# Width transform of a spectral block: one matmul over 128 rows, or two tiles of 64 rows into two PSUM banks

## The reference

```python
def _L0_conv_ref(x, w1, b1, w2, b2, bias_w, bias_b):
    bias = x @ bias_w.T + bias_b
    xb = x.reshape(B, H, W, nb, bs)
    xf = jnp.fft.rfftn(xb, axes=(1, 2), norm='ortho')
    xr, xi = (xf.real, xf.imag)
    r1 = jax.nn.relu(_block_mul(xr, w1[0]) - _block_mul(xi, w1[1]) + b1[0])
    i1 = jax.nn.relu(_block_mul(xr, w1[1]) + _block_mul(xi, w1[0]) + b1[1])
    r2 = _block_mul(r1, w2[0]) - _block_mul(i1, w2[1]) + b2[0]
    i2 = _block_mul(r2, w2[1]) + _block_mul(i1, w2[0]) + b2[1]
    out = jnp.fft.irfftn(jax.lax.complex(r2, i2), s=(H, W), axes=(1, 2), norm='ortho')
    return out.reshape(B, H, W, C) + bias
...
x = x + _L0_conv_ref(_gn(x), ...)
```

## Time and profile before

| | |
|---|---|
| runs, us | 493.98, 493.12, 493.60 (median 493.6) |
| the profiled execution | 493.3 us, span of its instructions 491.4 us |
| PE busy / weight loads busy | 462.8 us (94%) / 402.8 us (82%) |
| DVE busy | 327.0 us (67%) |
| ACT busy | 238.1 us (48%) |
| granted TensorE clock, mean | 0.982 of 2.4 GHz |

### The profile page before, as it was taken

How to read it: one execution, slowest core, us unless ns; L and a number is a source line. 1 busy time by engine, 2 the same in 40 slices (tenths; PEclk the granted TensorE clock), 3 DMA queues, 4 the chain that set the end, 5 groups by cost and what they waited for, 6 DMA issues and landing times.

```text
span 491.4 us, 15722 instructions
## 1 busy us (share of the span) xinstructions
PE 462.8 (94%) x6728; PEld 402.8 (82%) x6728; DVE 327.0 (67%) x769; ACT 238.1 (48%) x567; POOL 15.3 (3%) x16
## 2 busy tenths in 40 slices
PE   5476899999999999999999999999999999999996
PEld 5374688799888898799988998889987998887884
DVE  3695975578566884668756784668756785668524
ACT  3733483257542674247632683337732575425510
POOL 0030700000000000000000000000000000000000
PEclk9679999999999999999999999999999999999999
DMA  7640000250005100070003300070002500030003
GB/s 219 172 148 2 1 1 13 81 201 1 3 35 191 69 1 3 33 259 1 3 23 134 137 1 3 35 256 3 3 13 87 193 3 2 35 129 3 1 3 129
DMA packets 11637, 32.37 MB, mean 66 GB/s; under 512 B 4196, under 2 KB 5904, under 8 KB 11568
## 3 DMA queue, kind: packets, MB, share of 16 engines
q1 hardware_dynamic: 11568, 31.36, 18.1%
HBM read 15.63 MB, written 12.58 MB: 57 GB/s over the span
## 4 chain that ended last, share of the span: by engine, by line
PE 87%; DVE 5%; issue 3%; ACT 3%; DMA 1%; POOL 0%; DVEq 0%; SPq 0%; POOLq 0%; ACTq 0%
PE bank L521 87%; DVE r L989 1%; DVE rsum L982 1%; DMA x_sb<-in_x 1%; ACT y L813 1%; ACT junk L801 1%; DVE o_sb L1004 0%; DVE z L914 0%; ACT rho L848 0%; DVE extreme L1124 0%; ACT r L823 0%; DVE biasw L914 0%; ACT junk L804 0%; ACT z L833 0%; DVE rho L914 0%
## 5 line engine op out<-in xcount | busy, mean ns | idle before, releaser
L521 PE MATMUL bank<-w2s,rho 96*64 96x96 f16 (+1 forms) x3072 | 119.9, 247 | 0.0
L521 PEld LDWEIGHTS bank<-w2s,rho 96*64 96x64 f16 (+1 forms) x3072 | 107.9, 125 | 11.4 <-issue 11.3
L521 PE MATMUL bank<-biasw,y 128*128 128x384 f16 x576 | 105.4, 330 | 0.1
L521 PEld LDWEIGHTS bank<-biasw,y 128*128 128x128 f16 x576 | 78.6, 146 | 14.0 <-issue 0.2
L818 ACT ACTIVATE g<-bank 128x384 f16<-128x384 f32 x64 | 31.1, 485 | 98.3 <-PE bank L521 98.3
L996 DVE SCALAR_TENSOR_TENSOR g<-g,bank 128x384 f16<-128x384 f16 x64 | 35.4, 553 | 56.9 <-ACT g L818 56.9
L521 PE MATMUL bank<-w1R,y 128*128 128x192 f16 (+3 forms) x768 | 59.5, 228 | 4.4 <-ACT y L813 3.2
L833 ACT ACTIVATE z<-bank 128x384 f16<-128x384 f32 x72 | 35.3, 490 | 56.0 <-PE bank L521 56.0
L521 PEld LDWEIGHTS bank<-tab,x_sb 128*128 128x128 f32 x384 | 51.1, 201 | 9.1 <-issue 6.0
L521 PE MATMUL bank<-tab,x_sb 128*128 128x128 f32 x384 | 52.7, 285 | 6.0 <-DMA x_sb<-in_x 5.8
L914 DVE SCALAR_TENSOR_TENSOR z<-bank,z 128x384 f16<-128x384 f32 x72 | 39.7, 557 | 25.7 <-ACT z L833 24.7
(11 more groups left out here) (103 smaller groups left out, 421.5 us busy)
## 6 DMA issues: line engine op xcount, KB each, us to landing
x_sb<-in_x SPq DMA_DIRECT2D x16, 768.0 KB, 6.5
out<-o_sb SPq DMA_DIRECT2D x14, 768.0 KB, 4.1
y<-y SPq DMA_DIRECT2D x24, 128.0 KB, 2.7
out<-o_sb SPq DMA_DIRECT2D x8, 192.0 KB, 1.9
tab<-in_tab SPq DMA_DIRECT2D x1, 642.0 KB, 4.7
o_sb<-in_bias_wt SPq DMA_DIRECT2D x4, 144.0 KB, 2.7
b1s<-in_b1h SPq DMA_DIRECT2D x1, 384.0 KB, 5.2
o_sb<-in_w SPq DMA_DIRECT2D x2, 144.0 KB
```

Of the source, the lines that this page charges most:

```text
L521: return nc.tensor.matmul(o, lhsT, rhs, start=start, stop=stop, **kw)
```

## The change

Each float32 matmul of `p1` becomes two of half the size. One takes partitions 0 to 63 of `x_sb` (one pair of rows) as its stationary operand and 64 columns of the table, the other partitions 64 to 127 and their own 64 columns. They are row tiles of 64 rows in the array, and write two different banks. The zeros of the table are gone, and it is half as wide (TAB "width" 128 instead of 256 columns per partition).

An item now fills two banks: `y_bank[0:2]` for even `m`, `b_bank[0:2]` for odd `m`. `y_copy` becomes two activations of 256 columns each. The waits move with the banks: item 0 takes over the wait on `o_ready`, item 1 waits until `z` units 0 to 7 of the current image are evacuated, and `p4` takes its banks in another order.

```diff
-    width = by_unit(width.reshape(2, 128, 2, 4, 4, 4)).reshape(2, 128, 2, 64)
+
+    width = by_unit(width.reshape(2, 128, 2, 4, 4, 4)).reshape(2, 2, 64, 32, 2, 2)
+    width = np.stack([width[:, j, :, :, j, :] for j in range(2)], axis=1)
...
         def rho_bank(j, more):
-            return (*b_bank, *(y_bank if more else c_bank[0:2]))[j % 5]
+            return ((b_bank[2], *y_bank, *b_bank[0:2]) if more else (*b_bank, *c_bank[0:2]))[j % 5]
+
+
+        p1_banks = (y_bank, b_bank[0:2])
...
                 if m == 0 and not first:
                     pe.wait_ge(dve_step, NSTEP * (b - 1) + VAR_READ)
+                    pe.wait_ge(o_ready, 8 * b)
                 if m == 1 and not first:
-                    pe.wait_ge(o_ready, 8 * b)
+                    pe.wait_ge(zh_ready, 9 * b - 1)
+                    pe.wait_ge(zl_ready, 9 * b - 1)
                 if ct == 0:
                     pe.wait_ge(x_loaded[p][h], (b - p) * 8 + 16)
                 for i in range(4):
                     t = 4 * h + i
-                    src = x_sb[p][:, t, 128 * ct:128 * ct + 128]
-                    last = mm(y_bank[m % 2][:, 128 * i:128 * i + 128], src, width[:, 0 if t == 0 else 1, :], True, True)
+                    for j in range(2):
+                        rows = slice(64 * j, 64 * j + 64)
+                        last = mm(p1_banks[m % 2][j][:, 64 * i:64 * i + 64], x_sb[p][rows, t, 128 * ct:128 * ct + 128],
+                                  width[rows, 0 if t == 0 else 1, :], True, True)
                 last.then_inc(y_prod, 1)
...
-                    if j == 3 and more:
+                    if j in (1, 2) and more:
+                        pe.wait_ge(y_raw, Y_ITEMS * (b + 2) - 1)
+                    elif j == 3 and more:
                         pe.wait_ge(y_raw, Y_ITEMS * (b + 2))
                     elif j in (3, 4) and not more:
                         pe.wait_ge(spec_sum, 9 * b + 4 + j)
+                    elif j == 0 and more:
+                        pe.wait_ge(zh_ready, 9 * b + 9)
+                        pe.wait_ge(zl_ready, 9 * b + 9)
...
-                nc.scalar.activation(yraw[:, ct, :, :].rearrange("k a (m t) -> k (a m) t", t=TILES)[:, :, 4 * h:4 * h + 4],
-                                     y_bank[m % 2][:, :].rearrange("k (t m) -> k m t", t=4), ACT.Copy).then_inc(y_raw, 1)
+                columns = yraw[:, ct, :, :].rearrange("k a (c j x t) -> k (a c) j x t", j=2, x=2, t=TILES)
+                nc.scalar.activation(columns[:, :, 0, :, 4 * h:4 * h + 4],
+                                     p1_banks[m % 2][0][:, 0:256].rearrange("k (t c x) -> k c x t", t=4, x=2), ACT.Copy)
+                nc.scalar.activation(columns[:, :, 1, :, 4 * h:4 * h + 4],
+                                     p1_banks[m % 2][1][:, 0:256].rearrange("k (t c x) -> k c x t", t=4, x=2), ACT.Copy).then_inc(y_raw, 1)
```

More of the change, by code:

```diff
@@ L159 @@
 TABW = TAB16W = 0
-for _name, _wide in (("width", 256), ("own", 128), ("block3", 128), ("const", 64), ("rowscale", 1), ("coef", 5)):
+for _name, _wide in (("width", 128), ("own", 128), ("block3", 128), ("const", 64), ("rowscale", 1), ("coef", 5)):
     TAB[_name] = (TABW, TABW + _wide)
@@ L176, in put @@
         table[:a.shape[0], place[name][0]:place[name][1]] = a.reshape(a.shape[0], -1)
-    put("width", width.reshape(2, 128, 128).transpose(1, 0, 2))
+    put("width", width.reshape(2, 128, 64).transpose(1, 0, 2))
     put("height", H_SCALE * hgt.transpose(1, 0, 2))
```

## The result

The changed kernel takes 509.4 us (median of 4 runs, 508.39 to 509.84) against 493.8 (median of 4, 493.12 to 494.31) before: ratio 1.031, 95% interval 1.0298 to 1.0325. It is slower by 15.6 us, inside the stated range (492 to 522) and over the forecast of 501.9 by 7.5.

A forecast was written before the change was run, and what follows sets the result against it. PE, busy 94% of the span and unbroken in the steady chain, was taken as the bound. 36 items x 0.23 us = 8.3 us, start and first image nothing: 493.3 + 8.3 = 501.6, median 501.9 us; range 492 to 522.

The forecast's parts named there:

- The load sets the pace, side by side, nothing gained: In an item: 0.111 us per load sets the pace, both row tiles load together, 0.89 us as before.
- Two changes of shape per item: Between an item and its p3 neighbours: 0.25 us going in, 0.14 coming out, 0.23 us more per item.
- The start's six items stand in a row, with no change of shape: nothing: First group of items at the start: no added time; shorter table also taken as nothing, with 0.3 us as bound.
- So the first image pays nothing: First image's p3 stage: its six items cost nothing because PE waits there anyway; 1.4 us without that cover.
- The cover by DVE's waits: First image: PE's waits for rsum, 4.69 us before 46.40 and 1.05 before 55.85, hide the items' added time.
- A: The forecast case: tile loads side by side, two changes of shape per item; 499 to 508 us, chance 0.55.
- C: Rival: within a row tile a load isn't hidden under that tile's matmul; 512 to 522 us, chance 0.16.
- ACT and the banks: In the p3 stage: two copies take 0.78 us, ACT's 1.29 us fits a 1.61 us turn, PE doesn't wait for banks.
- E: Rival: a tile's load goes by the weights it holds, 0.056 us a pass; 483 to 487 us, chance 0.10.

The follow-up runs named there:

- e1: The kernel before with 64 moving columns instead of 128 in its width matmuls, half the transform left out: 495.0 us, ratio 1.0019.
- e2: The changed kernel with the tile of rows 0 to 63 alone, 8 loads and 8 matmuls per item instead of 16: 508.6 us.
- e3: The kernel before with the changed banks, waits, order of p4 and two activations per copy, its matmuls whole: 494.6 us, ratio 1.001.
- e4: The changed kernel with four tiles of 64 rows by 64 channels, 64 columns loaded and 64 moving: 490.3 us, ratio 0.9931.
- e5: The kernel before with two column tiles of 64 channels, all 128 rows and 128 moving columns: 502.7 us, ratio 1.0171.

## Why the prediction was right, and where it was off

- **The load sets the pace, side by side, nothing gained**: right, and shown three ways, by the loads two by two in the trace, by e1 and by e2. It rested on the 3-column matmuls, which any argument from moving columns would have missed.
- **Two changes of shape per item**: right in kind, and the size was near. Forecast 0.23 us an item, measured 0.26 (1.58 / 6). Going in is 0.26 us, as read from the earlier trace rows: the last `p3` matmul starts 0.16 us behind 111.96, at 112.12, the item at 112.38. Going out was taken as 0.14 from float16 tiles. Here the last matmul starts at 112.38 + 1.11 - 0.27 = 113.22 and the unit behind it at 113.42, 0.20 us. Float32 tile matmuls last 0.27 us in the trace, the float16 ones 0.207, which would account for it; no run tests that. In between, from the first matmul to the last, are 0.84 us where 8 x 0.111 = 0.89 stood, so two small errors partly cancel. 36 items make 9.5 us where 8.3 stood.
- **"The start's six items stand in a row, with no change of shape: nothing"**: wrong by 3.6 us in the two profiles, at least 2.3 against the others. The step counted the loads at their pace at full clock, which the kernel before reaches half way through this group. It never asked whether the changed items would reach it too. They don't. Nor did the shorter table bring the data earlier.
- **"So the first image pays nothing"**: wrong by 2.6 us. The cover by DVE's waits was read rightly: item 1 starts at 47.88, behind a wait of 3.46 us for `z`, and PE still waits 0.40 us for `rsum` behind it, with 1.05 us for the last unit gone. What followed ran at half clock for 17 us instead of 3.4. These two terms are 6.2 of the 7.4 us by which the forecast fell short, and the steady images the other 1.2. A's own range (499 to 508) had no room for them; the stated one had, for the sake of C, which did not happen. That the measured time lies in it is luck: the mechanism of A accounts for 9.5 of the 15.7 us, and the rest has a cause that no rival names.
- **ACT and the banks**: right. Each copy takes 0.38 us, and e3 puts the whole part at 0.5 us or less.
- **E, the faster side**: the reason against it held. A float32 load of 64 rows still passes at 0.11 us; it goes by its columns. The Trainium skill, TensorEngine Tiling, section Theoretical Speedup, has up to twice the speed for a dimension of 64 or less. Halving the rows alone gave nothing here; with 64 columns of load and 64 moving a pass does fall to 0.06 us (e4).

## What to carry to other kernels

Before splitting a matmul, ask for both of its sides, the columns loaded and the columns moved; a group with the same load and hardly any moving columns, if the trace has one, answers for the load at once. Here the two were within 5% of each other, so halving either alone gained nothing, and as tiles it only paid for the changes of shape, 0.26 us each way and back, while halving both gained 3.8 us (490.3 against 494.1), and 7.2 with the tiled items in pairs (487.2 against 494.4). And a sum made at full clock should be asked, for the start and for each place where PE has waited, whether the new work still brings the clock back.

## What the runs showed of the hardware

- TensorE can be busy without a pause for 10.5 us at the start and stay at 1.2 GHz, and busy for 98% of 17 us in the first image. At the start it happened with two row tiles, with one (e2) and with the whole array (e1), all with 64 columns moving behind a load of 128; in the kernel before (128 moving), with column tiles (e5) and with four tiles of 64 by 64 (e4) the clock rose to 2.4 GHz near 10 us. Why the one kind brings it up and the other does not, no run shows. Once the steady images have the full clock, none of these kernels loses it there, whatever its items.
- A float32 matmul of 128 moving columns streams in about 0.107 us (e1: 64 columns are 0.053; with a load of 64 columns, in e5, the pass is 0.11), against 0.111 for a float32 load of 128 columns. With 64 loaded and 64 moving a pass takes 0.06 us (e4); which of the two sets that is not shown.
- Two row tiles load and multiply side by side: a second tile costs 0.05 us in an image of 58 us (e2).
